# Sliding-window attention block on 8 cores: another order of the TensorE matmuls inside the score pieces and the P·V products

## The reference

```python
q = (x @ Wq.T).reshape(b, s, NH, D)          # 16 heads of 64
k = (x @ Wk.T).reshape(b, s, NKV, D)         # 4 heads, each shared by 4 query heads
v = (x @ Wv.T).reshape(b, s, NKV, D)
scores = 30 * tanh((q . k) * SCALE / 30)
mask = (j <= i) & (j > i - 1024)
o = softmax(where(mask, scores, -1e30)) @ v
x = layernorm(x + o @ Wo.T)
x = layernorm(x + relu(x @ quant(W1).T + b1) @ quant(W2).T + b2)   # ternary weights, 4096 wide
```

## Time and profile before

| | us |
|---|---|
| median of the runs | 1816.02 (1793.97 to 1838.07, 2 runs) |
| the profiled execution | 1790.52 |
| its span, slowest core (core 4) | 1788.9 |
| spans of the eight cores | 1748.2 to 1788.9 |
| TensorE busy, core 4 | 1198.6 (67%) |
| ScalarE busy, core 4 | 745.0 (42%) |
| VectorE busy, core 4 | 581.4 (33%) |

### The profile page before, as it was taken

The page is one execution under the profiler, slowest core; times in us unless marked ns, Lnnn a source line. Parts: engine busy times, 40 slices in busy tenths (PEclk is TensorE's granted clock), DMA queues, the critical chain, the costliest instruction groups (busy, mean ns, idle before and its releaser), DMA issues. The chain is left out here.

```text
span 1788.9 us, 24055 instructions; the slowest of 8 cores (1748.2 to 1788.9 us)
## 1 busy us (share of the span) xinstructions
PE 1198.6 (67%) x8196; PEld 657.2 (37%) x8196; DVE 581.4 (33%) x751; ACT 745.0 (42%) x668; POOL 226.4 (13%) x277
## 2 busy tenths in 40 slices
PE   5796467777676767676660099617777899367770
PEld 2353345555454545454530044202223344122220
DVE  0346434455555545555544600211100100212101
ACT  2232688888787868787600043200100234010100
POOL 1000000000101010111021000270000000720404
PEclk9798687678787878787875599858777899697875
DMA  9999542223232323232246322402221124131301
GB/s 143 212 258 291 132 97 87 83 70 109 84 112 89 108 80 113 81 117 83 83 136 176 104 71 77 142 0 71 94 71 65 36 77 130 71 141 71 141 24 47
DMA packets 127062, 186.69 MB, mean 104 GB/s; under 512 B 11104, under 2 KB 93024, under 8 KB 122848
## 3 DMA queue, kind: packets, MB, share of 16 engines
q1 hardware_dynamic: 103632, 131.14, 24.3%
q0 software_dynamic: 23312, 54.01, 11.7%
HBM read 161.53 MB, written 35.65 MB: 110 GB/s over the span
## 5 line engine op out<-in xcount | busy, mean ns | idle before, releaser
L550 ACT ACTIVATE Tst<-spsP 128x1024 f32<-128x1024 f32 x256 | 262.2, 1024 | 110.1 <-PE spsP L541 80.1
L1087 PE MATMUL f2ps<-hT,w2b 128*128 128x512 bf16 x1024 | 287.1, 450 | 2.6 <-DMA w2b<-w2q_t 1.5
L1041 PE MATMUL f1ps<-x2bf,w1b 128*128 128x512 bf16 x1024 | 226.3, 385 | 86.6 <-PEq L84 86.6
L569 ACT ACTIVATE Pst<-Tst,cm 128x4608 bf16<-128x4608 f32 x64 | 264.7, 4135 | 13.5 <-ACT Tst L556 13.3
L532 PE MATMUL spsP<-QT,KTd 64*128 64x128 bf16 x2304 | 134.4, 236 | 183.8 <-ACT Tst L550 163.5
L625 DVE RECIPROCAL den_sb<-pvd 128x256 f32<-128x256 f32 x64 | 112.5, 1758 | 278.1 <-PE pvd L609 278.1
L1114 ACT CAST t_bf<-x 128x512 bf16<-128x512 f32 x32 | 19.8, 618 | 410.1 <-DVE x L1107 410.1
L593 PE MATMUL pvd<-Pst,Vv 128*64 128x256 bf16 x1152 | 182.6, 393 | 2.1 <-DVE OTn L633 2.1
L1087 PEld LDWEIGHTS f2ps<-hT,w2b 128*128 128x128 bf16 x1024 | 116.0, 113 | 177.3 <-issue 98.4
L1041 PEld LDWEIGHTS f1ps<-x2bf,w1b 128*128 128x128 bf16 x1024 | 101.4, 99 | 211.8 <-issue 94.2
L532 PEld LDWEIGHTS spsP<-QT,KTd 64*128 64x128 bf16 x2304 | 76.3, 99 | 248.9 <-issue 248.9
(11 more groups left out here) (80 smaller groups left out, 962.2 us busy)
## 6 DMA issues: line engine op xcount, KB each, us to landing
qin<-w1T SPq DMA_DIRECT2D x64, 512.0 KB, 6.0
qin<-w2T SPq DMA_DIRECT2D x64, 512.0 KB, 5.4
w2b<-w2q_t SPq DMA_DIRECT2D x32, 1024.0 KB, 4.8
w1b<-w1q_t SPq DMA_DIRECT2D x64, 256.0 KB, 2.7
w1q_t<-qout POOLq DMA_DIRECT2D x32, 256.0 KB, 3.9
r1d<-r1f POOLq DMA_DIRECT2D x64, 128.0 KB, 3.7
w2q_t<-qout POOLq DMA_DIRECT2D x32, 256.0 KB, 3.5
outT<-x POOLq DMA_DIRECT2D x4, 2048.0 KB, 8.3
```

The costliest lines, as they stand in the source:

```text
L550: lambda e, ps=ps, kbp=kbp: e.activation(Tst[:, kbp * 1024:(kbp + 1) * 1024], ps[:, 0:1024], AF.Tanh, scale=1.0 / 240.0),
L569: lambda e, g=g: e.activation(Pst[g % 2][:, :], Tst[:, :], AF.Exp, bias=cm30[:, :], scale=30.0),
L1041: lambda e, dc=dc, nt=nt, wslot=wslot, pslot=pslot: e.matmul(f1ps[pslot][:, :], w1b[wslot][:, dc * 128:(dc + 1) * 128], x2bf[:, dc * 1024 ...
L1087: lambda e, fc=fc, nt=nt, wslot=wslot, pslot=pslot: e.matmul(f2ps[pslot][:, :], w2b[wslot][:, fc * 128:(fc + 1) * 128], hT[:, fc * 1024 + ...
```

## The change

It reorders instructions of TensorE and changes nothing else; their number, shapes, waits and signals stay as they are.

- Scores: `par` becomes the outermost loop of a piece. First all matmuls of the upper row half, by key block and head pair, then all of the lower half. In the two edge pieces the mask of a half follows right behind that half's matmuls, so that the order is half 0, mask 0, half 1, mask 1; before, both masks stood at the end.
- Products: `rel` becomes the outer loop and `par` the inner one, for L593 and for L609. The two column halves alternate from matmul to matmul.

```diff
-                        for a in range(na):
-                            kb = 2 * kbp + a
-                            ca = qt + kb
-                            for he in range(2):
-                                for par in range(2):
-                                    base = par * 64
+                        for par in range(2):
+                            base = par * 64
+                            for a in range(na):
+                                kb = 2 * kbp + a
+                                ca = qt + kb
+                                for he in range(2):
...
-                        if edge:
-                            moff = 0 if kbp == 0 else 512
-                            for par in range(2):
+                            if edge:
+                                moff = 0 if kbp == 0 else 512
                                 S.do("tensor",
                                      lambda e, ps=ps, par=par, moff=moff: e.matmul(
                                          ps[:, par * 512: par * 512 + 256],
...
-                    for par in range(2):
-                        for rel in range(NREL):
-                            ca = qt + rel
-                            vt = Vv[:, ca * 256 + kv * 64: ca * 256 + kv * 64 + 64]
+                    for rel in range(NREL):
+                        ca = qt + rel
+                        vt = Vv[:, ca * 256 + kv * 64: ca * 256 + kv * 64 + 64]
+                        for par in range(2):
...
-                    for par in range(2):
-                        for rel in range(NREL):
-                            ca = qt + rel
+                    for rel in range(NREL):
+                        ca = qt + rel
+                        for par in range(2):
```

More of the change, by code:

```diff
@@ L504, in emit_scores_acts @@
                         ps = spsP[(5 * g + kbp) % 2]
-                        for a in range(na):
-                            kb = 2 * kbp + a
-                            ca = qt + kb
-                            for he in range(2):
-                                for par in range(2):
-                                    base = par * 64
-                                    lhsT = KTd[base:base + 64,
-                                               kv * CTX + ca * 128:
-                                               kv * CTX + ca * 128 + 128]
+                        for par in range(2):
[3 more added lines that the diff above has]
+                                ca = qt + kb
+                                lhsT = KTd[base:base + 64,
+                                           kv * CTX + ca * 128:
+                                           kv * CTX + ca * 128 + 128]
+                                for he in range(2):
                                     hg = kv * 4 + 2 * he + par
```

## The result

The changed kernel takes 1813.23 us (median of 11 runs), the kernel before 1795.43 (10 runs, the two known at first among them). The ratios in this document leave out the runs in which the cores of one die showed a lower granted clock and the time was some per cent longer, and 1838.07, one of the two runs known at first, is such a run. The ratio is **1.0104, 95% interval 1.0065 to 1.0144**: 1% slower, and clear of no change.

The account below looks back on a forecast made before the run. TensorE's path decides the 10.22 us attention iteration, just above ScalarE's floor of 9.76. Terms -1 + 1.3 - 0.7 + 12.4 = +12 on the profiled 1790.5 give 1802 us, range 1766 to 1836.

Parts of the forecast that it names:

- The products' 6 places: Products already overlap, taking 24 places; alternating column halves makes 18, saving 0.66 us at full clock, 1.28 at half.
- The edge pieces: Score pieces 0 and 4: a mask between halves stops pairing, +0.42 us for piece 0, +0.49 for piece 4.
- Pieces 1 to 3: Scores without masks: nothing, or four more places (0.21 us full, 0.43 half clock), nearly hidden; taken as nothing.
- gain and loss nearly cancel inside an ordinary iteration: Attention iteration: net -0.03 us, +0.07 at full clock, -0.09 at half; some 41 iterations give about -1 us.
- the clock's term: After each long wait a half-clock stretch stays low, 3.3 us per group of eight; +12.4 us, chance 0.50.
- The four groups that were to change: Three more whole groups of eight iterations and most of a fourth, each slowed by a stretch that stays low.
- 12.4 + 1.3: Attention stage: +12.4 us for half-clock stretches that stay low, +1.3 us for five longer waits.
- the term for the first 27 iterations: Early attention iterations: no cost of their own, only a part of the sum's -1 us.
- the -1: Attention iterations: a net -0.03 us each over some 41 of them, about -1 us.
- the late last tanh: Piece 4's tanh at 511.15 instead of 510.79; the exp still ends just short of the limit, cover 0.1 us.
- the long waits: Five times TensorE waits at L742 for VectorE's L759; +0.25 us each, +1.3 us in all.

Follow-up runs that it names:

- e3: The changed kernel with both masks behind both row halves of an edge piece again; 0.9897 of the kernel before.
- e1: The kernel before with only the products reordered, column halves in turn, scores as they were; 0.9902 of the kernel before.
- e4: The kernel before plus nine overwritten idle-time matmuls of 64 rows per iteration, behind pieces 1, 2 and 3; 1.0008 of the kernel before.
- e5: The kernel before plus nine overwritten idle-time matmuls over the whole array (128 rows) per iteration, with other data; 0.9803 of the kernel before.

## Why the prediction was right or wrong

**Right.** The products' 6 places: 36 matmuls in 18 places; 3.08 us for 3.83, where the sum had 2.89. The edge pieces: 1.08 for 1.06 expected at full clock; at half clock 1.28 for 1.36, which makes the last tanh 0.27 us late where the prediction had 0.36. Pieces 1 to 3: unchanged, e3 equals e1. The verdict that gain and loss nearly cancel inside an ordinary iteration: iterations 13 to 16 last 10.22 to 10.23 us for 10.24 on the cores of the rows. And the clock's term, as a mechanism and as a number: the half-clock stretch that stays, the 1.85 us wait behind it, groups of eight at 92.2 us for 88.75. The four groups that were to change (27 to 34, 35 to 42, 51 to 58 and the rest) brought 13 us where 12.4 + 1.3 stood in the sum. That the clock stays low after a long wait because the new order opens holes in that stretch was argued, and no run tests it by itself.

**Wrong in size.** +18.7 us by the runs, +17.3 by the attention stretch, against +12. The step that failed is the term for the first 27 iterations. The sum gave them their part of the -1 (from iteration 10 on) and otherwise nothing; measured is +4.3 on the mean of the eight cores, and +6.3 on the two cores of the rows. Iterations 0 to 2 are 1.8 longer, 3 to 22 are 0.6 shorter, and 23 to 26 are 3.1 longer.

The last of these is the half-clock stretch again. It does not need a long wait to start it: it also came ahead of the long wait at 480.62, more than 200 us behind the one before, and in every core:

```profile
451.76 1.02 ACT L549 ACTIVATE Tst<-spsP 128x1024 f32<-128x1024 f32 x1 [1.98 <-PE spsP L540]
```

On this core iterations 24 and 25 last 11.88 and 11.12 us for 10.26 and 10.25: 2.5 us. On five of the eight it comes one iteration earlier. Iterations 0 to 2 grow mainly in the one long wait of this part, 8.90 us for 8.14. Why the extra stretch comes where it does stays open.

A second thing was overlooked there and in the end cost nothing on the mean. The prediction checked the late last tanh only against the late iterations, where TensorE's path just covers it; some early ones run at ScalarE's floor and have no such cover:

```profile
233.78 4.54 ACT L549 ACTIVATE Tst<-spsP 128x1024 f32<-128x1024 f32 x4
238.74 0.60 ACT L555 ACTIVATE Tst<-spsP 128x512 f32<-128x512 f32 x1 [0.42 <-PE spsP L540]
...
243.82 2.20 ACT L549 ACTIVATE Tst<-spsP 128x1024 f32<-128x1024 f32 x2
```

That is 10.04 us for an iteration that lasted 9.77 before, six times on this pair of cores: 1.6 us. But on three of the other cores the kernel before took 10.2 to 10.5 us in iterations 3 to 7, and no core of the changed kernel takes more than 10.1, so that over the eight cores the two nearly cancel.

**Wrong in what it was set against.** This is a second step that failed. The number, 1802, was the profiled execution's 1790.5 plus 12, and lay under the median then shown, 1816.02, the middle of 1793.97 and 1838.07. Read against that median it promises a gain of 0.8%, and measured is a loss of 1%; read against its own base, the profiled execution, its sign is the one measured. Against 1795.43, the better-known base, its own sum gives 1807, and measured is 1813.

**A small term that was mis-sized:** the long waits, +0.25 each in the sum, grew by about 0.35 (an iteration of 17.24 us became 17.59).

**Two rules that the prediction drew on.** The Trainium skill says that a change of tiling mode drains TensorE (TensorEngine Tiling (Array Packing), Key Properties). The rows of the changed kernel agree: at full clock the lower half starts 500.58 - 500.37 = 0.21 us behind mask 0, 0.10 more than the mask's place of 0.11. What the changes of mode cost by themselves no run shows: e3 takes two of them out of each edge piece and lets the halves run side by side again, and its 39 us hold both. The Trainium skill also says that matmuls start strictly in order (TensorE: Matmul & The Clock Gate, Part 3). The earlier trace rows show a later line starting first, and in piece 3 above the two halves are four matmuls apart in the program and take no longer than with alternating ones, so here the measurement decides against that rule.

## What to carry to other kernels

Before reordering matmuls so that array halves pair up, look in the timeline for a later line that starts ahead of an earlier one: TensorE may be pairing them already, and what is won is the rest (here 24 places became 18, not 36). Keep work that uses the whole array out of the middle of half-array work. And where TensorE waits in short turns for another engine, count the half-clock stretches that follow: here they were worth 28 us, the reordering of the products 23, and whole-array work in the gaps paid for itself.

## What the runs showed of the hardware that I had not expected

- Nine idle-time matmuls of 64 rows to an iteration left the granted clock from 500 to 560 us at 0.83 (0.84 without); nine of 128 rows, as many and as wide but with other data, raised it to 0.93.
- A busier TensorE did not go with a higher granted clock: 48.8 of 60 us busy at 0.83 (e4), 46.2 of 60 at 0.93 (e5). Matmuls take longer at the lower clock, which is part of the 48.8.
- Costs of separate edits did not add: +10 and +14 alone, +39 together; and -23 with +69 gave +17.
